# Fewer steps in the routing softmax: a summed exponential on ScalarE and one doubled split on VectorE

## The reference

```python
x = _layernorm(x + attention(x, qkvw, qkvb, ow, ob))     # 32 heads of 16
x = _layernorm(x + cross_attention(x, ctx, ctx, mask))   # 32 query heads, 8 key/value heads
x = _layernorm(x + ffn(x))

# ffn, with E = 8 experts:
router_logits = xf @ gate_w.T                            # [tokens, 8]
routing = softmax(router_logits, axis=1)
in_scale = routing @ in_channel_scale
out_scale = routing @ out_channel_scale
out = xf * in_scale @ sign(weight).T * out_scale + bias
```

## Time and profile before

| | |
|---|---|
| three timed runs | 402.18, 406.38, 407.63 us; median 406.38 |
| profiled execution, its own time | 409.41 us |
| its span, first to last instruction | 407.6 us |
| instructions | 7606 |
| mean clock granted to TensorE | 0.864 of full speed |
| around the core's span | 1.8 us (409.41 - 407.6) |

### The profile page before, as it was taken

How to read it: one execution, slowest core, us unless ns; L and a number is a source line. 1 busy time by engine, 2 the same in 40 slices (tenths; PEclk the granted TensorE clock), 3 DMA queues, 4 the chain that set the end, 5 groups by cost and what they waited for, 6 DMA issues and landing times.

```text
span 407.6 us, 7606 instructions
## 1 busy us (share of the span) xinstructions
PE 341.6 (84%) x2661; PEld 244.0 (60%) x2661; DVE 267.6 (66%) x974; ACT 153.7 (38%) x293; POOL 113.0 (28%) x203
## 2 busy tenths in 40 slices
PE   1693789997889999997999999879899965699563
PEld 1692556795647758975567499666556743444342
DVE  0968653558757648688785497878756777804444
ACT  3852135420144854302375733023755520046220
POOL 3362400131240314433422155421121431000321
PEclk9998568998895999996999999959999976579755
DMA  8948800167570001784510026955000155000001
GB/s 282 374 152 241 183 4 6 56 191 220 145 185 5 12 22 57 206 248 122 167 55 5 0 82 192 260 134 160 5 14 2 44 145 142 4 2 2 0 1 51
DMA packets 26703, 42.59 MB, mean 104 GB/s; under 512 B 8153, under 2 KB 18529, under 8 KB 24361
## 3 DMA queue, kind: packets, MB, share of 16 engines
q1 hardware_dynamic: 26393, 41.58, 36.1%
q10 hardware_dynamic: 272, 0.52, 0.3%
HBM read 29.32 MB, written 12.32 MB: 102 GB/s over the span
## 4 chain that ended last, share of the span: by engine, by line
PE 65%; DVE 20%; issue 5%; DMA 4%; ACT 3%; POOL 2%; SPq 0%; POOLq 0%; DVEq 0%; ACTq 0%
DVE x L778 8%; PE bank_a L883 7%; PE bank_a L884 7%; PE bank_a L885 7%; PE bank_a L962 4%; PE bank_a L932 4%; PE bank_b L1027 4%; PE bank_b L1016 4%; PE bank_a L949 3%; PE bank_b L1017 3%; PE bank_b L1019 3%; PE bank_b L1062 3%; PE bank_b L1063 3%; DVE nma L714 2%; PE bank_b L1004 2%
## 5 line engine op out<-in xcount | busy, mean ns | idle before, releaser
L778 DVE CUSTOM_DVE_ANT_0 x<-bank_b,mraw 128x128 f32<-128x128 f32 x256 | 59.0, 287 | 9.3 <-PE bank_b L1004 2.6
L596 ACT ACTIVATE pb<-bank_b 128x512 f32<-128x512 f32 x64 | 37.6, 600 | 61.7 <-PE bank_b L1019 44.0
L588 ACT ACTIVATE pa<-bank_a 128x512 f32<-128x512 f32 x64 | 37.5, 597 | 26.2 <-PE bank_a L949 13.8
L714 DVE TENSOR_REDUCE nma<-bank_a 128x4 f32<-128x512 f32 x64 | 39.9, 681 | 6.7 <-PE bank_a L932 6.5
L883 PE MATMUL bank_a<-xH,wH 128*128 128x256 f32 x128 | 37.6, 294 | 3.4 <-DVE xL L686 3.4
L1016 PE MATMUL bank_b<-idr,mH 128*128 128x512 f32 x64 | 36.9, 576 | 0.6 <-DVE nmb L778 0.5
L884 PE MATMUL bank_a<-xL,wH 128*128 128x256 f32 x128 | 37.0, 289 | 0.0
L885 PE MATMUL bank_a<-xH,wL 128*128 128x256 f32 x128 | 36.9, 288 | 0.0
L1004 PE MATMUL bank_b<-kx,qx 96*128 96x128 bf16 x256 | 27.0, 252 | 11.5 <-DVE nmb L778 8.9
L932 PE MATMUL bank_a<-ks,qs 96*128 96x128 bf16 x256 | 25.2, 250 | 11.0 <-DMA ks<-scr_k 8.9
L1004 PEld LDWEIGHTS bank_b<-kx,qx 96*128 96x128 bf16 x256 | 18.5, 112 | 20.9 <-DVE nmb L778 12.9
(11 more groups left out here) (160 smaller groups left out, 738.5 us busy)
## 6 DMA issues: line engine op xcount, KB each, us to landing
wraw<-in_L_attn_attn_qkvw_dram SPq DMA_DIRECT2D x3, 1024.0 KB, 8.7
scr_q<-qp SPq DMA_DIRECT2D x8, 384.0 KB, 3.1
qs<-scr_q SPq DMA_DIRECT2D x8, 384.0 KB, 4.5
scr_k<-kp SPq DMA_DIRECT2D x8, 384.0 KB, 4.2
ks<-scr_k SPq DMA_DIRECT2D x8, 384.0 KB, 4.9
scr_x<-xp SPq DMA_DIRECT2D x8, 384.0 KB, 2.7
qx<-scr_x SPq DMA_DIRECT2D x8, 384.0 KB, 4.0
qs<-scr_q SPq DMA_DIRECT2D x8, 256.0 KB, 4.6
```

What stands on the lines that cost most here:

```text
L714: dve.tensor_reduce(nma[:, b, 4 * j:4 * j + 4], pa_bank(i, *step)[:].rearrange("p (m t) -> p m t", m=KT), AX.X, ALU.max, negate=True).then ...
L778: last = dve.tensor_tensor_reduce(x2[:, b, r * P:(r + 1) * P], pb_bank(i, *step)[:, r * P:(r + 1) * P], mraw[:], -1.0, -LOWEST, ALU.add, A ...
```

## The change

ScalarE's exponential of step rt also gives the sum over its eight columns and writes it to sl, so the sum on DVE goes away. The rounding to fp32r no longer goes to rtH but straight to both high blocks of rts, with one instruction whose input is rt read twice. One subtraction, again with rt read twice, writes both low blocks; it now waits for the rounding through route_step. The tile rtH is gone. Constants of the semaphore waits follow the smaller count of steps (3 a group and sequence, before 5).

```diff
-        rtH = sb("rtH", [P, GB, E], F32R)
...
                 elif thread == "B" and name == "rt":
                     b = step[1]
                     act.wait_ge(top_made[b], i + 1)
-                    act.activation(el[:, b, :], pb_bank(i, *step)[:, 0:E], ACT.Exp, bias=nl[:, b:b + 1]).then_inc(*rb.is_empty(i, *step))
+                    act.activation(el[:, b, :], pb_bank(i, *step)[:, 0:E], ACT.Exp, bias=nl[:, b:b + 1], accum_out=sl[:, b:b + 1]).then_inc(*rb.is_empty(i, *step))
...
                     rb.wait_emptied(dve, i, "rt", b)
-                    dve.tensor_reduce(sl[:, b:b + 1], el[:, b, :], AX.X, ALU.add).then_inc(route_step[b], 1)
-                    dve.wait_ge(route_step[b], 5 * i + 1)
                     dve.reciprocal(rl[:, b:b + 1], sl[:, b:b + 1]).then_inc(route_step[b], 1)
-                    dve.wait_ge(route_step[b], 5 * i + 2)
+                    dve.wait_ge(route_step[b], 3 * i + 1)
                     dve.tensor_scalar(rt[:, b, :], el[:, b, :], rl[:, b:b + 1], None, ALU.mult).then_inc(route_step[b], 1)
-                    dve.wait_ge(route_step[b], 5 * i + 3)
-                    dve.tensor_copy(rtH[:, b, :], rt[:, b, :]).then_inc(route_step[b], 1)
-                    dve.wait_ge(route_step[b], 5 * i + 4)
-
-                    high = rtH[:, b, :].bitcast(F32)
-                    for k in (0, 2):
-                        dve.tensor_copy(rts[:, b, k, :], high)
-                        last = dve.tensor_tensor(rts[:, b, k + 1, :], rt[:, b, :], high, ALU.subtract)
-                        last.then_inc((route_step if k == 0 else route_made)[b], 1)
+                    dve.wait_ge(route_step[b], 3 * i + 2)
+
+                    whole = rt[:, b, :].rearrange("p (o e) -> p o e", o=1).broadcast_to([P, 2, E])
+                    dve.tensor_copy(rts[:, b, 0:4:2, :].bitcast(F32R), whole).then_inc(route_step[b], 1)
+                    dve.wait_ge(route_step[b], 3 * i + 3)
+                    dve.tensor_tensor(rts[:, b, 1:4:2, :], whole, rts[:, b, 0:4:2, :], ALU.subtract).then_inc(route_made[b], 1)
```

## The result

The changed kernel takes 401.89 us (median of 15 runs, 398.06 to 404.11) against 405.94 us for the kernel before (15 runs, 402.18 to 408.14). The ratio is 0.9896, with a 95% interval of 0.9867 to 0.9925: 4.2 us or 1.0% faster, between 3.0 and 5.4. So the direction and the range held, and the gain was about twice the forecast.

A forecast was written before the change was run, and what follows sets the result against it. TensorE, busy 84% of the span, bounds the kernel, so VectorE savings count only where it waits. Gains of 0 + 0.20 + 0.20 + 1.49 = 1.9 us take the median 406.38 to 404.5 us, range 400.9 to 407.3.

The forecast's parts named there:

- TensorE's wait for the route: TensorE's transpose of rts (L1048) waits for VectorE's last subtraction: four times, 11.5 us, forecast to shrink to near 9.2.
- The route gets 0.40 us shorter: VectorE's instruction chain from the sum to TensorE's transpose: 1.25 us down to 0.85 per place, before ScalarE's cost.
- the dear bound: Upper bound for VectorE's 16-column rounding and subtraction: twice the busy time, 0.17 us more each, against 0.01 taken.
- ScalarE's read-out at 0.20: Writing out the sum behind ScalarE's exponential delays the reciprocal by 0.20 us, between bounds of 0 and 0.27.
- the same picture: Group 1, sequence 1: TensorE's wait of 3.46 us ends with the route, so gain 0.20 us as in group 2.
- Group 0 gives nothing, the wait moves to L940: Group 0, sequence 1: TensorE's next instruction waits for POOL's L477 instead, so the transpose's 0.40 us gains 0.
- Group 3 gives 1.49: Last route: read-out hidden, 0.40 us shorter, and a 1.09 us copy stall beside POOL's L544 goes too.
- Rival (a): Last route: the new subtraction starts after POOL's L544 and stalls; sum 0.2 us, time 406.2; chance 0.12.
- It moves as a whole, at half clock already: Everything behind the last transpose follows in TensorE's order at half clock, so it shifts earlier by the full 1.49 us.
- Rival (c): Half-clock stretch at 187.1, 6.8 us long, disappears through a shorter wait: 3.4 us more gained, 401.1; chance 0.15.
- (b): Gains in groups 1 and 2 lost at the next wait, the end's stall gain not repeating: about 0, 406.4; chance 0.14.
- (d): Slower: the half-clock stretch behind group 1's route gets longer, costing 5.0 us, time 409.5; chance 0.10.

The follow-up runs named there:

- c3: Kernel before with the tile rtH declared behind rT, so three small tiles lie 64 bytes lower, nothing else; 406.11 us, ratio 1.0026.
- e3: Kernel before with only the last of the eight routes (group 3, sequence 1) changed; 402.24 us, ratio 0.9926.
- e4: Kernel before with all routes but the last changed, the last keeping its stall beside POOL; 404.73 us, ratio 0.9950.
- e6: Changed kernel with VectorE's last route ahead of zf of sequence 0, and zH's four matmuls ahead of zL's; 400.5 us, ratio 0.9865.
- e8: Changed kernel with six useless matmuls in TensorE's waits before the transpose in groups 0 to 2, sequence 1; 397.9 us, ratio 0.9824.
- e9: e6 with the same six useless matmuls as e8; 398.57 us, ratio 0.9832.
- e1: Kernel before with only the sum moved to ScalarE, copies and subtractions kept; 404.34 us, ratio 0.9927.
- e2: Kernel before with only the doubled rounding and subtraction, the sum staying on VectorE; 401.33 us, ratio 0.9914.
- c1: Kernel before once more, unchanged, as a control; 405.23 us, ratio 1.0007.
- e7: Kernel before with six useless matmuls in TensorE's waits before the transpose in groups 0 to 2, sequence 1; 403.59 us, ratio 0.9886.

## Why the prediction was right or wrong

**TensorE's wait for the route is where the change counts, and only in sequence 1: right.** The waits stayed four in number and shrank from 11.5 to 8.7 us (9.2 forecast): by 0.32 in group 0, 0.67 in group 1, 0.31 in group 2 and 1.49 in group 3.

**The route gets 0.40 us shorter: right.** It is 0.40 to 0.41: 326.67 to 327.35 + 0.17 is 0.85, as summed. The wide forms cost 0.01 each; the rounding and the subtraction took 0.17, and the dear bound can go. By the Trainium skill's rule (VectorE: DVE Perf Modes, section "The DRAIN you can't avoid") it would have been 0.65, an estimate from the durations in the trace; the trace does not agree with it.

**ScalarE's read-out at 0.20: mis-sized.** It is busy for 0.19, but overlaps the exponential and delays the reciprocal by 0.09. The routes of groups 1 and 2 give 0.32 each, not 0.20. The step that failed was the choice of a bound by likeness to a second ScalarE instruction, as though such a one had to wait for the first to end.

**Group 1 is "the same picture" as group 2: mis-sized.** The route's part is the same 0.32, but the wait shrank by 0.67, because VectorE's work ahead of it also came 0.35 us earlier, which the prediction had left as it was. Most of it lasts. From the first exponential to the sixth, which takes in groups 0 and 1, it is 183.41 to 183.53 us in before, c3 and e3, and 182.99 to 183.17 in the changed kernel (twice), e4 and e6, with the same stretches of half clock: about 0.4 us less, where 0.32 - 0.11 would be 0.2.

**Group 0 gives nothing, the wait moves to L940: right, and a little worse.** The transpose came 0.31 us earlier behind the exponential, and the next instruction 0.11 later. The timeline of the changed kernel, answering to the earlier trace rows:

```profile
183.15 0.54 DVE L746 TENSOR_SCALAR x<-x,mva,rsa 128x512 f32<-128x512 f32 x1
...
183.38 0.27 PE L1042 MATMUL bank_b<-idf,rts 128*32 128x128 f32 x1 [2.32 <-DVE rts L813]
183.39 0.40 POOL L476 TENSOR_TENSOR npb<-nrb,npb 128x32 bf16<-128x32 f32 x1
183.90 0.12 PEld L934 LDWEIGHTS bank_b<-idb,npb 128*96 128x96 bf16 x1 [0.46 <-issue]
183.93 0.23 PE L934 MATMUL bank_b<-idb,npb 128*96 128x128 bf16 x1 [0.29 <-POOL npb L476]
```

VectorE's normalisation L746 now starts before POOL's last piece L476 instead of after it, and L476 takes 0.40 instead of 0.28; it takes 0.40 or 0.41 in all six profiles with the whole change in group 0 (the changed kernel twice, e4, e6, e8, e9). This looks like the stall of the last route with the parts exchanged; it was not tested by itself.

**Group 3 gives 1.49: right to 0.01,** and so was the reason. The Trainium skill (GPSIMD Engine Reference, section "Key points") names two SBUF inputs as a cause of contention with GpSimd; e1 and e2 agree, with 1.23 and 1.26 us. Two inputs are not needed, though: the copy that was held in the kernel before has one. Rival (a) was the sharpest of the rivals: e2 is exactly its case, with the subtraction 0.03 us late and held for 1.26. It did not come true because the rounding cost 0.01 and not 0.17.

**"It moves as a whole, at half clock already": this step failed.** Rows 11 said that the clock was at half in the tail; I took it for a fixed condition. In the profiles of the kernels whose last route has no stall, the clock came back to full during the last matmuls in five of six (the changed kernel twice, e6, e8, e9; not e3). Of the seven with the stall (before, c1, c3, e1, e2, e4, e7) it did in none; there it is 14.17 us from the transpose to the end, each time, and in e3 too. Why an earlier start lets the clock rise is only argued: the same matmuls run, with a stall of 1.1 us less ahead of them.

**Rival (c) had the right kind of cause at too low a chance (0.15), and the wrong place.** The stretch that it named, behind group 0, stayed at 6.8 us, and the one behind group 1 at 10.3. The one behind group 2 went from 10.2 to 6.8, and the one at the end was cut off by the clock's return. Over many executions it acts as a mean, 103 us at half clock down to 94, worth 2.2 us. My argument against it, that a wait shorter by 0.2 to 0.4 us is much the same wait, held in groups 0 and 1 and failed in group 2, where 0.31 us less of waiting went with 3.4 us less at half clock in four profiles out of four. (b) fell: the direct gain was there at equal clock. (d) was the wrong sign.

In sum: the direct term was 1.9 forecast, 2.0 to 2.4 by the traces, 1.9 ± 0.2 and 2.7 ± 0.4 by the runs; the missing 2 us went with the clock, which the forecast had put at nothing. That the 1.9 comes so close to 2.0 owes something to luck: the two places put too low by 0.12 each and the 0.11 lost in group 0 cancel in part, and the 0.35 us of group 1 were not in it.

**What stays open.** Why e3, which changes only the last 20 us of the program, spent 10 us less at half clock than the kernel before: the tail can hold a few us of it at most. In its profile the time from the sixth exponential to the eighth is 56.08 us against 57.86 in the kernel before and 57.90 in c3, so 1.8 us were won by the clock ahead of the first instruction that e3 changes. Its ratio's interval reaches from 1.3 to 4.7 us faster, and its own direct part is 1.5, so a part may be chance. The controls exclude a bias of the comparison. Nothing here excludes that the clock's part of a single kernel is off by 1 us or more, and so it is shown that the clock's part was there in both comparisons of the change, but not how much of it the shorter waits cause.

## What to carry to other kernels

Look at the start times of VectorE and GpSimd side by side where a short VectorE instruction shows a duration far above its median: 0.2 us cut from the work ahead of it can be worth 1.1 us more, or nothing, depending on which of the two starts first. Where the matrix engine waits and its clock falls behind the wait, the wait can cost twice, and it is worth trying to shorten it or to fill it with useless matmuls: here 0.31 us less of waiting in group 2 went with 3.4 us less at half clock, while in groups 0 and 1 waits shorter by 0.32 and 0.67 us left the half clock as long as it was. Compare such kernels at equal clock too, by a line through all runs, before a difference of half a per cent is put down to the edit.

## What the runs showed of the hardware

- A ScalarE exponential that also gives its sum is two instructions, 0.27 and 0.19 us busy, which overlap; a waiting VectorE instruction starts 0.39 instead of 0.30 us after the first one's start.
- A VectorE copy, or a subtraction of two SBUF inputs, of only 8 or 16 columns that starts 0.03 to 0.07 us after a GpSimd subtraction of 128x512 lasts 1.23 to 1.26 us, until GpSimd is done; one that starts 0.01 us before it lasts 0.16.
- Six useless 128x512 matmuls in each of three waits of TensorE took the mean granted clock of the kernel before from 0.878 to 0.893; the ratio of the times was 0.9886, the medians over all executions 403.59 and 405.12 us. The changed kernel with them had a clock of 0.904 and 397.9 us.
- In this kernel one us of TensorE at half clock costs about 0.26 us of span, by a line through 156 executions.
